# Newton norm groups spread over an attention tail, the order of head and tails, and an exponential of a constant behind three square roots

## Chip, core and metric

The kernel runs on one core of a Trainium2 chip. The metric is the device time of one execution in microseconds (us), lower is better. The engines of the core are PE (matrix multiplications and transpositions), DVE (vector), ACT (scalar: activations, copies, and the table loads that some activation functions need), POOL (a second, slower vector engine) and SP, which here only issues DMAs. Each engine works through its own list of instructions in order and waits at semaphores.

## What is computed

Four cross-attention layers run one after the other over 8 sequences of 128 rows by 256 columns, in float32. Each has projections, scores, a softmax and a weighted sum; L1, L2 and L3 end in an MLP with GELU. Of L0 the change touches only the first microseconds. What matters besides is the normalisation of rows, which stands in front of every part:

```
def layer_norm(x, w, b):
    mu = jnp.mean(x, axis=-1, keepdims=True)
    var = jnp.mean(jnp.square(x - mu), axis=-1, keepdims=True)
    return (x - mu) * jax.lax.rsqrt(var + EPS) * w + b
...
attn = jax.nn.softmax(scores, axis=-1)
out = jnp.einsum('bhqk,bhkd->bhqd', attn, v)
...
y = jax.nn.gelu(y @ fc_w + fc_b, approximate=True)
```

L1 uses a norm without the mean (`rmsnorm`, EPS 1e-06) between its attention and its MLP.

## The kernel before

The program is written as five instruction lists, one for each engine, that walk the same planned order of events. Projections in full precision are made of three fp32r products each (`three`, L768 to L770: high part by low, low by high, high by high), so every weight and every activation is split: ACT writes the rounded high part, DVE the rest. PE's general results go through two PSUM banks in turn, `ps` banks 6 and 7 ("general banks"): PE may fill one again only when the engines that read its last content are done, so the order of `j_bank` users on PE, ACT and DVE is one order.

**Head.** L0 runs in steps of 4 units. For a step, PE gathers stacked queries and keys (L1108 to L1111), ACT copies them (L1407), SP (for the first step ACT too) moves rows of the keys by DMA (L660), PE makes the scores (L1128), DVE takes maxima (L1816), POOL and a product with a rounded identity, `identR` (PE L1118), turn these into a correction, and PE and ACT make the exponentials (L1137, L1417). Rows, identity and a mask are loaded by three DMAs (L706 to L708) that SP issues behind the key moves of step 1. DVE waits for all three, adds a bias row to the values (L1806) and then writes `identR` (L1810).

**Attention of L1 and L3.** `att_order` lists units: 64 in L1 (4 iterations of 4 steps of 4), 32 in L3 (4 iterations of 4 steps of 2). A unit is: PE scores `S` (L897 in L1, L903 in L3), DVE maxima (L1619), ACT exponentials (L1274, which also sums), DVE reciprocal (L1570), POOL product (L1867), PE transposition `T` (L913), a copy by ACT (even units, L1285) or DVE (odd ones, L1632), and the product with the values `PV` (L936). There are two banks for scores and two for transpositions. Once for each step PE gathers queries `pq` (L855) and keys `pk` (L862, L865), which ACT (L1256, L1266) and DVE (L1616) write back. After an iteration ACT and DVE split the result (L1291, L1635) and the output projection `WO` follows; DVE adds it to the residual (L1641) and takes statistics (L1485).

**The norm** comes in three events: `nS` (DVE aggregates the statistics, L1496, and writes the variance; ACT takes the square root, L1214), `nX` (DVE reciprocal, L1505, and the scaled rows, L1508 or L1510, one instruction for each sequence) and `nT` for each pair of sequences (PE transposes, L802; ACT applies weight and bias, L1226 or L1228; DVE splits, L1524 and L1525). The square root and the exponential need different tables, as does GELU, so each switch has an `ACT_TABLE_LOAD` ahead of it. `GROUPS` says which pairs share an `nS`. The first group of the norm behind the attention, `L1r` in L1 and `L3nm` in L3, is worked in the attention's last units. There the table of extra events reads as follows (`total` is the number of units):

```
    first, rest, sqrt = {"L1": (total - 24, total - 4, 10), "L3": (10, total - 3, 5)}[ph]
...
    put(total - sqrt, "nS", after, 0)
    put(total - sqrt + 1, "nX", after, 0)
```

So `nS` comes in unit 54 of L1 and 27 of L3. The first MLP products `up` (12 products each; GELU on ACT L1369, split on DVE L1723 and L1724) stand in units `total`, `total + 1` and `total + 4`, among the last transpositions. Weights arrive in packs (DMA L690) and are split by `take` (ACT L1205, DVE L1475).

**Seams.** Before L2 (`L2n1`), in its middle (`L2n2`) and before L3 (`L3n1`) the last group's `nS` is the last square root ahead of exponentials; their table is loaded ahead of the first one (L1329 in L2, L1274 in L3). Keys and queries of L2 are written by ACT (L1312, L1306), scores are L988, maxima L1680, reciprocals L1688, transpositions L997.

## Time and profile before

| | us |
|---|---|
| three runs, median | 1166.39 |
| lowest, highest | 1165.26, 1166.6 |
| the profiled execution | 1168.75 |
| its span, first to last instruction | 1167.0 |
| PE busy, share of the span | 1061.5, 91% |
| DVE busy | 728.7, 62% |
| ACT busy | 716.2, 61% |
| POOL busy | 316.8, 27% |

The profiled execution is 0.20% above the median, and 1.75 us of it lie outside the span. PE is busy for most of the time; the parts where it is not are the head, the attention of L1 and L3 and the seams. The views used below are the timeline, which gives each instruction's start and length and the idle time ahead of it with its releaser; the chain of waits; and the busy time of all engines in a stretch, with the clock that TensorE was granted (1.00 is 2.4 GHz, 0.50 is 1.2 GHz).

### The profile page before, as it was taken

The page shows a single profiled execution, that of the slowest core. Times are in us where ns is not written, and L with a number is a line of the kernel's source. Part 1 is how long each engine was busy: PE and PEld are TensorE (multiplying, and loading weights), DVE is VectorE, ACT ScalarE, POOL GpSimd, SP SyncE. Part 2 cuts the span into 40 slices and gives each one's busy share as a digit, 9 for nine tenths or more (in the row PEclk, how much of TensorE's full clock was granted, in tenths as well). Part 3 has the DMA queues.
Part 4 walks back from the last instruction along what each step waited for, and adds up shares of the span by engine and source line. Part 5 has one row for each costly group of instructions (what it writes and reads, how often), then busy time and mean ns, then how long its engine had stood idle before and what let it go on. Part 6 is the DMA issues. An engine that isn't in the chain of part 4 may idle for free.

```text
span 1167.0 us, 24069 instructions
## 1 busy us (share of the span) xinstructions
PE 1061.5 (91%) x8248; PEld 936.3 (80%) x8248; DVE 728.7 (62%) x1755; ACT 716.2 (61%) x2080; POOL 316.8 (27%) x440
## 2 busy tenths in 40 slices
PE   7989897799979999999999979999999989778788
PEld 6767676577759889999998869999998979667588
DVE  6787584677786645555555645555555585767773
ACT  2777765677884465656655556565665552689852
POOL 5242533666540022211111103111111112243311
PEclk8999999899999999999999999999999999999899
DMA  5211111011101021111101001011111110100100
GB/s 169 70 43 46 24 33 42 16 29 25 44 26 46 19 91 46 47 46 47 46 17 71 28 22 45 25 46 46 46 46 37 32 60 1 49 17 19 48 10 28
DMA packets 29853, 48.09 MB, mean 41 GB/s; under 512 B 6627, under 2 KB 20389, under 8 KB 29734
## 3 DMA queue, kind: packets, MB, share of 16 engines
q1 hardware_dynamic: 29638, 46.49, 13.0%
q8 instruction: 68, 1.11, 0.4%
q14 instruction: 51, 0.42, 0.1%
q10 hardware_dynamic: 96, 0.07, 0.0%
HBM read 36.54 MB, written 1.05 MB: 32 GB/s over the span
## 4 chain that ended last, share of the span: by engine, by line
PE 65%; DVE 13%; ACT 10%; issue 7%; POOL 2%; SPq 1%; DMA 1%; ACTq 0%; DVEq 0%; POOLq 0%
PE ps L768 14%; PE ps L769 13%; PE ps L770 13%; PE ps L1012 4%; PE ps L988 4%; PE ps L1150 3%; ACT pt L1274 2%; PE ps L997 2%; DVE nm L1816 2%; PE ps L913 1%; DVE nmax L1619 1%; PE ps L1128 1%; PE ps L1137 1%; PE ps L936 1%; POOL pt L1867 1%
## 5 line engine op out<-in xcount | busy, mean ns | idle before, releaser
L1867 POOL TENSOR_TENSOR pt<-pt,prec 128x256 f32<-128x256 f32 (+1 forms) x224 | 181.3, 810 | 622.9 <-DVE prec L1688 501.1
L1329 ACT ACTIVATE pt<-ps,nmax 128x129 f32<-128x129 f32 x256 | 92.4, 367 | 100.7 <-DVE nmax L1680 99.9
L1475 DVE TENSOR_TENSOR rs<-wraw,rs 128x256 fp32r<-128x256 f32 (+2 forms) x116 | 68.7, 594 | 125.5 <-ACT rs L1205 125.1
L768 PE MATMUL ps<-rs 128*128 128x256 f32 x480 | 142.8, 298 | 4.1 <-DVE rs L1702 2.8
L769 PE MATMUL ps<-rs 128*128 128x256 f32 x480 | 135.9, 283 | 0.0
L770 PE MATMUL ps<-rs 128*128 128x256 f32 x480 | 135.8, 283 | 0.0
L1274 ACT ACTIVATE pt<-ps,nmax 128x256 f32<-128x256 f32 (+1 forms) x256 | 105.3, 425 | 40.3 <-DVE nmax L1619 39.9
L768 PE MATMUL ps<-ht,rs 128*128 128x256 f32 (+1 forms) x304 | 107.5, 354 | 9.0 <-DVE ht L1525 3.0
L770 PE MATMUL ps<-ht,rs 128*128 128x256 f32 (+1 forms) x304 | 100.9, 332 | 0.0
L769 PE MATMUL ps<-ht,rs 128*128 128x256 f32 (+1 forms) x304 | 100.9, 332 | 0.0
L768 PEld LDWEIGHTS ps<-rs 128*128 128x128 f32 x480 | 91.9, 191 | 7.9 <-DVE rs L1702 4.8
L1702 DVE SCALAR_TENSOR_TENSOR rs<-ps,col,rs 128x256 fp32r<-128x256 f32 x128 | 61.9, 483 | 53.4 <-ACT rs L1346 53.4
L769 PEld LDWEIGHTS ps<-rs 128*128 128x128 f32 x480 | 92.0, 192 | 0.0
L770 PEld LDWEIGHTS ps<-rs 128*128 128x128 f32 x480 | 91.9, 191 | 0.0
L768 PE MATMUL ps<-rs,ct 128*128 128x256 f32 x288 | 86.4, 300 | 3.4 <-ACT rs L1256 1.5
L1816 DVE TENSOR_REDUCE nm<-ps 128x2 f32<-128x512 f32 x128 | 82.6, 680 | 6.3 <-PE ps L1128 6.2
L988 PEld LDWEIGHTS ps<-fs 128*128 128x128 f32 x512 | 76.1, 191 | 10.2
L1619 DVE TENSOR_REDUCE nmax<-ps 128x2 f32<-128x512 f32 (+1 forms) x96 | 65.7, 685 | 29.5 <-PE ps L903 24.1
L1369 ACT ACTIVATE fs<-ps,col 128x256 f32<-128x256 f32 x96 | 40.2, 472 | 68.4 <-PE ps L770 67.2
L1417 ACT ACTIVATE pt<-ps 128x512 f32<-128x512 f32 x128 | 73.1, 599 | 13.3 <-PE ps L1137 11.6
L770 PE MATMUL ps<-rs,ct 128*128 128x256 f32 x288 | 80.9, 281 | 0.0
L769 PE MATMUL ps<-rs,ct 128*128 128x256 f32 x288 | 80.9, 281 | 0.0
(206 smaller groups left out, 2999.4 us busy)
## 6 DMA issues: line engine op xcount, KB each, us to landing
wraw<-in_packs SPq DMA_DIRECT2D x52, 512.0 KB, 3.7
rs<-rs SPq DMA_DIRECT2D x222, 32.0 KB, 1.9
bvr<-in_l2rows SPq DMA_DIRECT2D x16, 256.0 KB, 4.5
rs<-rs SPq DMA_DIRECT2D x96, 16.0 KB
row<-in_rows SPq DMA_DIRECT2D x2, 640.0 KB, 4.9
XH<-in_packs SPq DMA_DIRECT2D x2, 512.0 KB, 4.2
out<-X SPq DMA_DIRECT2D x4, 256.0 KB, 2.1
X<-in_x SPq DMA_DIRECT2D x3, 256.0 KB, 3.2
```

Of the source, the lines that this page charges most:

```text
L768: nc.tensor.matmul(dst, w[0], m[1], start=start, stop=False)
L769: nc.tensor.matmul(dst, w[1], m[0], start=False, stop=False)
L770: return nc.tensor.matmul(dst, w[0], m[0], start=False, stop=stop)
L988: last = nc.tensor.matmul(ps[:, S_BANK + g % 2, b * D:b * D + P + 1], qT[:, hh % 3, 2 * b2 + b, :], kT[:, hh % 3, 2 * b2 + b, :], start=Tr ...
L1274: last = nc.scalar.activation(prob[:, i % PROBS, h * keys:(h + 1) * keys], ps[:, SCORE_BANKS[ph][i % len(SCORE_BANKS[ph])], h * keys:(h + ...
L1329: last = nc.scalar.activation(prob[:, g % PROBS, k * D:k * D + P + 1], ps[:, S_BANK + g % 2, k * D:k * D + P + 1], ACT.Exp, bias=nmax[:, g ...
L1417: nc.scalar.activation(pt[:, i % L0_PTS, :], ps[:, L0_X[i % len(L0_X)], :], ACT.Exp, scale=Q0_SCALE).then_inc(Z["ex"], 1)
L1475: last = nc.vector.tensor_tensor(dst[1], src, f32(dst[0]), ALU.subtract)
L1619: nc.vector.tensor_reduce(nmax[:, i % 4, 0:nh], ps[:, SCORE_BANKS[ph][i % len(SCORE_BANKS[ph])], :].rearrange("p (h n) -> p h n", h=nh), A ...
L1702: nc.vector.scalar_tensor_tensor(cc[1][:, hd, two, :], ps[:, O_BANK + g % 2, 0:D].rearrange("p (b n) -> p b n", b=2), C(f"L2bv{p // PAIRS ...
L1816: nc.vector.tensor_reduce(nm[:, s % 3, im, 2 * p:2 * p + 2], ps[:, L0_S[i % len(L0_S)], :].rearrange("p (h n) -> p h n", h=2), AX.X, ALU.m ...
L1867: nc.gpsimd.tensor_tensor(pr, pr, prec[:, u % 4, 0:nh].unsqueeze(2).broadcast_to([P, nh, keys]), ALU.mult)\
```

## The change

1. **Newton roots.** For the first groups of `L1r` and `L3nm` (`ROOTS`) the square root on ACT and the reciprocal on DVE go. DVE computes 1/sqrt by itself: in `nS` two instructions that make a first guess from the bits of the number, and three rounds (`refine`) of three small instructions, each waiting for the one before. Two rounds stand in a new event `nR`, the third ahead of the first scaled rows.
2. **Spread.** `nX` of these groups is cut by pairs: in L1 `nS` in unit 54, `nR` in 55, pairs in 56, 57, 58 and their `nT` in 58, 60, 63 (before: 57, 60, 63); in L3 `nS` in 24, `nR` in 25, pairs in 26 and 27, `nT` in 27 and 29 (before `nS` in 27, `nX` in 28, `nT` in 30 and 31).
3. **Tails.** `up` 0, 1, 2 move from `total`, `total + 1`, `total + 4` to `total + 2`, `total + 4`, `total + 5`.
4. **Head.** SP issues the three loads behind the key moves of step 0 in place of step 1, and DVE writes `identR` ahead of the bias addition.
5. **Tables.** Behind the last square root of `L2n1`, `L2n2` and `L3n1` (`WARM`) ACT takes the exponential of one constant column into a tile that nobody reads, so that the table of the exponential is loaded there.

```diff
+ROOTS = {("L1r", 0), ("L3nm", 0)}
+ROOT_SEED = 0x5F3759DF - (1 << 30) - (1 << 22)
+WARM = {("L2n1", 1), ("L2n2", 1), ("L3n1", 1)}
...
-    first, rest, sqrt = {"L1": (total - 24, total - 4, 10), "L3": (10, total - 3, 5)}[ph]
+    first, rest = {"L1": (total - 24, total - 4), "L3": (10, total - 3)}[ph]
...
-    put(total - sqrt, "nS", after, 0)
-    put(total - sqrt + 1, "nX", after, 0)
-    for n, k in enumerate(GROUPS[after][0]):
-        put(total - sqrt + 3 + (3 if ph == "L1" else 1) * n, "nT", after, k)
+    sums, scale, turn = {"L1": (54, (56, 57, 58), (58, 60, 63)), "L3": (24, (26, 27), (27, 29))}[ph]
+    put(sums, "nS", after, 0)
+    put(sums + 1, "nR", after, 0)
+    for k in GROUPS[after][0]:
+        put(scale[k], "nX", after, 0, k)
+    for k in GROUPS[after][0]:
+        put(turn[k], "nT", after, k)
     for k in range(2):
-        put(total + k, "up", 0, k)
+        put(total + 2 + 2 * k, "up", 0, k)
         put(total + k, "w", f"{ph}w2_0", 2 * k, 2)
         put(total + 5 + k, "w", f"{ph}w2_1", 2 * k, 2)
-    put(total + 4, "up", 0, 2)
+    put(total + 5, "up", 0, 2)
...
                         if e == "pp":
                             key_blocks(i)
-                            if i == 1:
+                            if i == 0:
...
-                if e == "nS":
-                    act.wait_ge(n["stat"], k + 1)
+                if e == "nS" and (name, k) not in ROOTS:
+                    act.wait_ge(n["stat"], rooted(name, k))
...
+                if e == "nX" and (name, k) in WARM:
+                    nc.scalar.activation(warm[:, 0:1], eps[:, 0:1], ACT.Exp)
...
+            def refine(g):
+
+                link(nc.vector.tensor_tensor(sd[:, 2, g], sd[:, 3, g], sd[:, 3, g], ALU.mult))
+                link(nc.vector.tensor_tensor(sd[:, 2, g], sd[:, 2, g], sd[:, 0, g], ALU.mult))
+                link(nc.vector.scalar_tensor_tensor(sd[:, 3, g], sd[:, 2, g], 1.5, sd[:, 3, g], ALU.add, ALU.mult))
...
+                    if (name, k) in ROOTS:
...
+                        link(nc.vector.tensor_scalar(sd[:, 0, g], power, 1e-6 if name == "L1r" else 1e-5, -0.5, ALU.add, ALU.mult))
+                        link(nc.vector.tensor_scalar(sd[:, 3, g].bitcast(I32), sd[:, 0, g].bitcast(I32), -0.5, float(ROOT_SEED),
+                                                     ALU.mult, ALU.add))
...
+                elif e == "nR":
+                    refine(g)
+                    refine(g)
                 elif e == "nX":
...
+                    if (name, k) in ROOTS:
+                        if pair == GROUPS[name][k][0]:
+                            refine(g)
...
                         dve.wait_ge(d_in, 16 * 3)
+                        nc.vector.tensor_copy(identR, ident[:, :]).then_inc(ident_r, 1)
...
-                    if i == 0:
-                        nc.vector.tensor_copy(identR, ident[:, :]).then_inc(ident_r, 1)
```

The order of the instructions shows the change at three places. A name in brackets is a semaphore that the instruction waits for; `x3` means three more of the same.

**DVE in L1's last units.** Before, from the statistics on (`mv`, `sd` are statistics and factors, `nmax` the maxima of a unit, `prec` its reciprocals, L1508 the scaled rows):

```order
L1499 TENSOR_TENSOR sd<-mv 128x6 [waits vector_chain]
L1500 TENSOR_TENSOR sd<-sd,mv 128x6 [waits vector_chain]
L1619 TENSOR_REDUCE nmax<-ps 128x2 [waits L1_sm]
L1570 RECIPROCAL prec<-psums 128x2 [waits L1_nm,L1_ex]
L1505 RECIPROCAL sd<-sd 128x6 [waits L1r_sq]
L1508 TENSOR_SCALAR XH<-XH,sd 128x256 [waits vector_chain]
L1508 TENSOR_SCALAR XH<-XH,sd 128x256 x5
L1619 TENSOR_REDUCE nmax<-ps 128x2 [waits L1_sm]
L1570 RECIPROCAL prec<-psums 128x2 [waits L1_nm,L1_ex]
L1632 COPY pt<-ps 128x512 [waits L1_pm,L1_tm]
```

With the change (its own line numbers: L1524 and L1525 are the first guess, L1497 to L1499 a round, L1655 the maxima, L1544 the scaled rows):

```order
L1524 TENSOR_SCALAR sd<-sd 128x6 [waits vector_chain]
L1525 TENSOR_SCALAR sd<-sd 128x6 [waits vector_chain]
L1655 TENSOR_REDUCE nmax<-ps 128x2 [waits L1_sm,vector_chain]
L1606 RECIPROCAL prec<-psums 128x2 [waits L1_nm,L1_ex]
L1497 TENSOR_TENSOR sd<-sd 128x6
L1498 TENSOR_TENSOR sd<-sd 128x6 [waits vector_chain]
L1499 SCALAR_TENSOR_TENSOR sd<-sd 128x6 [waits vector_chain]
L1497 TENSOR_TENSOR sd<-sd 128x6 [waits vector_chain]
L1498 TENSOR_TENSOR sd<-sd 128x6 [waits vector_chain]
L1499 SCALAR_TENSOR_TENSOR sd<-sd 128x6 [waits vector_chain]
L1655 TENSOR_REDUCE nmax<-ps 128x2 [waits L1_sm,vector_chain]
L1606 RECIPROCAL prec<-psums 128x2 [waits L1_nm,L1_ex]
```

Further down stand the third round and two scaled rows, and the other four come in pairs behind the next two maxima. So seven instructions between one maximum and the next become six small ones, two more stand ahead of the first maximum, and three more and two rows ahead of the third.

**ACT in L3's last units.** Before, from the exponentials of unit 27 to those of unit 28 and what follows (L1274 exponentials, L1285 copy, L1291, L1256, L1266 results of `pq`, `pk` and the split):

```order
L1274 ACTIVATE pt,psums<-ps,nmax 128x128 [waits L3_tm,L3_mx]
L1274 ACTIVATE pt,psums<-ps,nmax 128x128 x3
L1285 COPY pt<-ps 128x512 [waits L3_pm,L3_tm]
L1214 ACT_TABLE_LOAD
L1214 ACTIVATE sd<-sd,eps 128x4 [waits L3nm_stat]
L1274 ACT_TABLE_LOAD [waits L3_tm]
L1274 ACTIVATE pt,psums<-ps,nmax 128x128 [waits L3_mx]
L1274 ACTIVATE pt,psums<-ps,nmax 128x128 x3
L1291 CAST rs<-ps 128x512 [waits L3_done,L3_pm]
L1256 ACTIVATE rs<-ps,col 128x512 [waits general_bank_filled,L3_sm]
L1266 CAST rs<-ps 64x2x128 [waits general_bank_filled,L3_sm]
L1274 ACTIVATE pt,psums<-ps,nmax 128x128 [waits L3_tm,L3_mx]
```

With the change (L1288 exponentials, L1299 copy, L1240 the affine step of a pair):

```order
L1288 ACTIVATE pt,psums<-ps,nmax 128x128 [waits L3_tm,L3_mx]
L1288 ACTIVATE pt,psums<-ps,nmax 128x128 x3
L1299 COPY pt<-ps 128x512 [waits L3_pm,L3_tm]
L1240 ACTIVATE XH<-ps,col 128x256 [waits general_bank_filled]
L1240 ACTIVATE XH<-ps,col 128x256
L1288 ACTIVATE pt,psums<-ps,nmax 128x128 [waits L3_tm,L3_mx]
L1288 ACTIVATE pt,psums<-ps,nmax 128x128 x3
L1305 CAST rs<-ps 128x512 [waits L3_done,L3_pm]
L1270 ACTIVATE rs<-ps,col 128x512 [waits general_bank_filled,L3_sm]
L1280 CAST rs<-ps 64x2x128 [waits general_bank_filled,L3_sm]
L1288 ACTIVATE pt,psums<-ps,nmax 128x128 [waits L3_tm,L3_mx]
L1288 ACTIVATE pt,psums<-ps,nmax 128x128 x3
```

Two table loads and a square root went, and the affine step of the first pair, before behind unit 30, stands in their place.

**ACT at the seam into L2.** Before (L1214 square root, L1310 and L1312 a key block, L1226 affine steps):

```order
L1214 ACTIVATE sd<-sd,eps 128x2 [waits L2n1_stat]
L1310 ACTIVATE fs<-ident,col 128x4 [waits general_bank_filled]
L1312 ACTIVATE fs<-ps,col 128x4x128
L1226 ACTIVATE XH<-ps,col 128x256 [waits general_bank_filled]
L1226 ACTIVATE XH<-ps,col 128x256
L1205 CAST rs<-wraw 128x1024 [waits pack_loaded0,L1m_out]
L1306 ACTIVATE fs<-ps,l2q 128x512 [waits general_bank_filled]
L1226 ACTIVATE XH<-ps,col 128x256 [waits general_bank_filled]
```

With the change (L1229 is the exponential of the constant):

```order
L1226 ACTIVATE sd<-sd,eps 128x2 [waits L2n1_stat]
L1324 ACTIVATE fs<-ident,col 128x4 [waits general_bank_filled]
L1326 ACTIVATE fs<-ps,col 128x4x128
L1229 ACT_TABLE_LOAD
L1229 ACTIVATE warm<-eps 128x1
L1240 ACTIVATE XH<-ps,col 128x256 [waits general_bank_filled]
L1240 ACTIVATE XH<-ps,col 128x256
L1217 CAST rs<-wraw 128x1024 [waits pack_loaded0,L1m_out]
L1320 ACTIVATE fs<-ps,l2q 128x512 [waits general_bank_filled]
L1240 ACTIVATE XH<-ps,col 128x256 [waits general_bank_filled]
```

The load that stood ahead of the first L1329 now stands between the key block and the affine step.

## Rows read from the trace of the kernel before

**Rows 1.** The page: its head line, and its chain of work that ended last, by engine.

```profile
span 1167.0 us, 24069 instructions
...
PE 65%; DVE 13%; ACT 10%; issue 7%; POOL 2%; SPq 1%; DMA 1%; ACTq 0%; DVEq 0%; POOLq 0%
```

**Rows 2.** The chain of waits in the head, in order of time: start, us, what.

```profile
18.68 3.90 DMA mraw<-in_mask_s
```

**Rows 3.** Timeline of the head: start, us, engine, line, operation, count, [idle before].

```profile
13.13 4.40 SPq L660 DMA_DIRECT2D rs<-rs  x6
...
22.70 0.49 DVE L1806 TENSOR_TENSOR fs<-ps,row 128x128 f32<-128x128 f32 x2 [1.63 <-DMA mraw<-in_mask_s]
...
23.66 0.69 PE L1118 MATMUL ps<-rs 128*128 128x128 f32 x2 [2.77 <-DVE rs L1810]
...
24.91 0.29 PEld L1128 LDWEIGHTS ps<-rs 128*128 128x128 f32 x1 [0.33 <-DMA rs<-rs]
```

**Rows 4.** Busy time by stretch: us, PE, PEld, DVE, ACT, POOL, granted clock, DMA share, GB/s.

```profile
24.00:30.00 6.00, 6.00 (x23) 5.24 (x23) 5.63 (x14) 2.06 (x4) 0.65 (x3) 0.51 0.65 205
...
1094.00:1102.00 8.00, 4.99 (x33) 3.78 (x34) 5.23 (x11) 8.00 (x35) 2.47 (x3) 0.57 0.01 3
1112.00:1120.00 8.00, 6.01 (x42) 5.81 (x43) 5.08 (x9) 2.51 (x6) 2.06 (x2) 0.79 0.01 2
```

**Rows 5.** Timeline, last units of L1's attention: DVE and ACT.

```profile
324.16 0.68 DVE L1619 TENSOR_REDUCE nmax<-ps 128x2 f32<-128x512 f32 x1
...
324.60 1.28 ACT L1274 ACT_TABLE_LOAD   x1
...
324.83 0.17 DVE L1505 RECIPROCAL sd<-sd 128x6 f32<-128x6 f32 x1
...
325.04 2.46 DVE L1508 TENSOR_SCALAR XH<-XH,sd 128x256 f32<-128x256 f32 x6
325.89 0.47 ACT L1274 ACTIVATE pt<-ps,nmax 128x256 f32<-128x256 f32 x1
...
327.42 0.68 DVE L1619 TENSOR_REDUCE nmax<-ps 128x2 f32<-128x512 f32 x1
```

**Rows 6.** Timeline, end of L1's attention on PE.

```profile
351.30 0.64 PE L936 MATMUL ps<-pt,fs 128*32 128x128 f32 x16 [2.25 <-DVE pt L1632]
...
356.37 0.36 PE L768 MATMUL ps<-ht,rs 128*128 128x256 f32 x1
```

**Rows 7.** Timeline, seam from L1's MLP to L2.

```profile
407.80 0.67 ACT L1312 ACTIVATE fs<-ps,col 128x512 f32<-128x512 f32 x1
...
411.85 0.47 PE L768 MATMUL ps<-ht,rs 128*128 128x512 f32 x1
```

**Rows 8.** Timeline, second half of L2 begins.

```profile
693.34 1.28 ACT L1329 ACT_TABLE_LOAD   x1
...
698.57 0.46 PE L997 MATMUL ps<-ident,pt 128*128 128x128 f32 x2 [1.84 <-POOL pt L1867]
```

**Rows 9.** Timeline, first unit of L3's attention.

```profile
1011.13 0.69 DVE L1619 TENSOR_REDUCE nmax<-ps 128x4 f32<-128x512 f32 x1 [1.72 <-PE ps L903]
```

**Rows 10.** Timeline, last units of L3's attention: ACT and PE.

```profile
1090.84 1.28 ACT L1214 ACT_TABLE_LOAD   x1
...
1092.44 1.28 ACT L1274 ACT_TABLE_LOAD   x1
...
1093.74 0.37 ACT L1274 ACTIVATE pt<-ps,nmax 128x128 f32<-128x128 f32 x1
...
1097.01 0.77 PE L903 MATMUL ps<-rs 128*128 128x256 f32 x2 [4.24 <-DVE rs L1616]
...
1101.60 0.41 ACT L1274 ACTIVATE pt<-ps,nmax 128x128 f32<-128x128 f32 x1
```

**Rows 11.** Timeline, end of L3's attention on PE.

```profile
1113.99 0.42 PE L936 MATMUL ps<-pt,fs 128*32 128x128 f32 x8 [2.31 <-DVE pt L1632]
...
1118.81 0.28 PE L768 MATMUL ps<-ht,rs 128*128 128x256 f32 x1
```

More of the change, by code:

```diff
@@ L100, with rooted @@
           "L3n1": ((0, 1, 2), (3,)), "L3nm": ((0, 1), (2, 3))}
+ROOTS = {("L1r", 0), ("L3nm", 0)}
+ROOT_SEED = 0x5F3759DF - (1 << 30) - (1 << 22)
+WARM = {("L2n1", 1), ("L2n2", 1), ("L3n1", 1)}
 NORMS = ["ctx", "lat", "L1r", "L2n1", "L2n2", "L2nm", "L3n1", "L3nm"]
+def rooted(name, k):
+    return sum((name, j) not in ROOTS for j in range(k + 1))
 def first_order():
@@ L458, in build @@
         eps = sb("eps", [P, 2])
+        warm = sb("warm", [P, 1])
         nm = sb("nm", [P, 3, 2, 4])
@@ L1487, in stats, with norm_step @@
                     link(last)
-            def norm_step(e, name, k):
+            def norm_step(e, name, k, pair=None):
                 n = N[name]
-                if e in ("nS", "nX"):
+                if e in ("nS", "nR", "nX"):
                     src = XH if name == "L1r" else X
```

18 lines of the change are left out of this document (12 added, 6 removed).

## Prediction

> **What bounds the kernel.** First the page: a span of 1167.0 us, and a chain that ended last of which PE has 65%, DVE 13%, ACT 10% [rows 1]. PE is the limit almost everywhere, so an edit pays only where PE stands still, or runs at the lower clock, and only as much as that. I went through the chain of waits and then the timeline at the places that the diff touches. What the reader is to see there: in the head PE stands 2.77 us for `identR` [rows 3]; in the tails of L1's and L3's attention ACT or DVE is full while PE waits, up to 4.24 us at once [rows 10]; at the seams PE waits for short chains through ACT and DVE. The stretches view adds the clock: 0.51 in the head's 24 to 30, 0.57 and 0.79 in L3's tail [rows 4].
>
> The sum is made against the profiled span of 1167.0; that execution took 1168.75, 0.20% above the median of 1166.39, to which I apply the difference unscaled.
>
> **Head.** Before, SP issues six key moves from 13.13 to 17.53 [rows 3], then the three loads, the last at 18.68 with 3.90 us to land [rows 2]; DVE is idle 1.63, goes on at 22.70, and PE at 23.66 [rows 3]. With the loads behind two moves, they start 4 × 4.40/6 = 2.9 us earlier (the estimate counts SP's own wait for step 1 as issue time). `identR` is done before the bias work, so PE could go on about 2 us earlier. The price: key moves of step 1 are issued some 1.3 us later by SP and queue behind the large row load. What is late next is the transfer for step 2, which even now holds PE's weight load until 24.91 [rows 3]. It is issued only a few tenths earlier, since it waits for ACT's stacks. So the gain at 24.91 is 0.3 to 0.9 us; it can grow behind that, as PE was at half clock from 24 to 30 with a busy share of 6.00 in 6.00 [rows 4], but DVE was busy 5.63 of these 6.00 and would catch it at once. I take **-1.0**, bounds -2.5 (DVE's idle time of 1.63 and the transfer's 0.9) and 0 (the step 1 moves take it all back).
>
> **L1's tail.** Removed on ACT: a load (1.28), a square root, a load (1.28) [rows 5]. But look at who is late. The maxima of unit 55 end at 324.84, the exponential starts at 325.89, so the loads cost 1.0 there, and the maxima of unit 56 come at 327.42 only because DVE was scaling six rows for 2.46 us [rows 5]. DVE is the limit for four units. A linked small instruction costs 325.04 - 324.83 = 0.21 us from start to start [rows 5]. Added are 2 + 9 of them, 2.3 us, less one reciprocal of 0.21: **2.1 us more on DVE**, and the 2.46 us of scaling stay. I moved the timeline on: exponentials of unit 55 at 325.3 (0.6 earlier), of 56 about 0.8 earlier, then of 57 some 0.8 later, because third round and two rows stand ahead of its maxima, and the carry at unit 63 is 1.1 late (0.5 to 1.3).
>
> The end is reordered. Before, two `up` groups of some 1.45 us each stand among the last transpositions; the last copy is late on DVE, and PE idles 2.25 us until 351.30 [rows 6]. Now they stand behind the last transposition, one of them behind the last `PV`, so `PV` comes about 1.2 earlier with the carry in, but one more `up`, and the split ahead of `WO`, follow it. The point that I compare is the group that began at 356.37 [rows 6]: it comes 0.8 late by my hand. L1's tail: **+0.8**, bounds -1.5 (DVE's additions fit into its idle time) and +2.5 (two loads' worth comes back as a carry of all 2.1 us).
>
> **L3's tail.** The same edits, but here ACT is the limit: 8.00 busy of 8.00 us [rows 4]. The loads at 1090.84 and 1092.44, with the root between them, hold the exponentials of unit 28 until 1093.74: the removed piece is 1093.74 - 1090.84 = 2.9 us [rows 10]. Guess and first rounds move to units 24 and 25, where DVE has idle time; third round and two rows (0.6 + 0.7) stand ahead of the maxima of 27 and hold it 0.9. The affine step of pair 0 (two instructions, 1.0) now stands ahead of the exponentials of 28, that of pair 1 ahead of 30. By hand: exponentials of 28 start 1.0 earlier, PE's unit 30, which waits 4.24 until 1097.01, 0.55 earlier, those of 31 within 0.2 of 1101.60 [rows 10], but now both affine steps lie behind ACT and not ahead. From there no `up` stands between the last transpositions and no split ahead of the last copies: the last `PV`, at 1113.99 after 2.31 us idle [rows 11], comes at about 1108.4 to 1109; then `up`, split and `WO`, two `up`, and the group that began at 1118.81 [rows 11] begins at about 1114.3, 4.5 earlier. The old stretch had clock 0.79 [rows 4]; the new one has emptier time before its products, and I give 0.5 back for that. **-4.0**, bounds -5.5 and -1.5.
>
> **Seams.** The load is 1.28 and the exponential of one column some 0.2, together 1.5, moved ahead of affine steps. At L2n1, ACT's key block ends at 408.47 (407.80 + 0.67) and the affine step follows at once; DVE's split, its value block and PE's group at 411.85 [rows 7] hang on it one behind another: **+1.6** there. The load taken away later stood beside a PE that was busy; I find 0.4 of idle time behind it. Net **+1.2**, bounds 0 and +3.0 (the low clock follows the new gap). At L2n2 the load at 693.34 is in the chain that ends in 1.84 us of PE idle at 698.57 [rows 8]; ACT has room behind its root, so **-1.0**, bounds -2.7 and 0. At L3n1 the maxima end at 1011.82 [rows 9], when the old load was just through: **0**, to +0.3.
>
> Here the Trainium skill speaks to the load. The trace first: 324.60 plus 1.28 is 325.88, and the exponential starts at 325.89 [rows 5]. The page "ScalarE: Activation LUTs", section "What ACT_TABLE_LOAD costs", gives a load of about 1283 ns and a drain of about 1380 ns behind it for every switch. By that each of the four loads removed would give back 1.4 us more; the trace has the first figure and not the second, and it decides.
>
> The skill also speaks against the change. The page "VectorE: DVE Perf Modes", section "Rules for kernel authors", says of chained operations to keep their number small, not their semaphores. By that rule eleven small operations are the wrong coin for one square root. My terms above already charge each by its row.
>
> **Sum.** -1.0 + 0.8 - 4.0 + 1.2 - 1.0 + 0 = -4.0: 1166.4 - 4.0 = **1162.4 us** (0.34% faster; the span 1163.0). A measurement of this kernel can tell about 0.2%, 2.3 us, from no change.
>
> **Rivals.**
> - *The gaps go and the clock stays up* (0.20). The low clock of the head [rows 4] follows an idle PE; if that gap is short, the products there run at full rate. Head -2.5, L1 -1.0, L2n1 0.5, L2n2 -2.5, L3 -5.0: -10.5, **1155.9**. Against it: a transfer still holds PE at 24.91.
> - *The expected gain is given back behind it* (0.22). DVE's linked instructions hold the maxima in both tails, and the end of L3 hangs on copies that queue on DVE: head -0.5, L1 +1.5, L2n1 +1.2, L2n2 -0.5, L3 -2.5: -0.8, **1165.6**.
> - *Slower: the low clock moves onto dense products* (0.09). Before, much of it fell on stretches where ACT was the limit (0.57 with ACT full [rows 4]). With the `up` groups behind the last transposition PE is emptier ahead and then has 6 us of products in a row, which at half rate cost 3 more, in L1 and in L3, and 2 at the new gap of L2n1: 8 against -4.0, **1170.4**. It decides if at least three such stretches fall there.
> - *The constant's exponential loads nothing, or a load stays ahead of the exponentials as well* (0.01): the instruction order shows one load, at the new place. Only the seams would be off, by 1 us.
>
> **Chances.** Forecast 0.48, rivals 0.20, 0.22, 0.09, 0.01. Faster by over 0.2%: 0.44 of the forecast's 0.48, 0.20, 0.03 of the second: **0.67**. Slower by over 0.2%: **0.08** (third rival nearly whole). Within: **0.25**. The range for 8 in 10 takes in most of the first two rivals: **1155.5 to 1167.0**. The forecast's own is 1159 to 1165.
>
> **What would show it.** In the new trace: PE goes on in the head before 22.5 and waits for the transfer near 24.4; between the maxima of units 55 and 56 of L1 six instructions 0.21 apart, and maxima of 57 later than before; in L3 no load between exponentials, PE's wait at unit 30 under 4 us, last `PV` to the group behind `WO` and two `up` more than 5 us; at L2n1 about 1.5 us more idle ahead of the group that stood at 411.85; at L2n2 under 1 us in place of 1.84. The forecast is wrong if linked instructions cost clearly more than 0.21, if L3's last `PV` is not at least 4 us earlier, or if the clock's low stretches fall on the `up` groups.

## The result and the profile after

The changed kernel took **1168.71 us** (median of 20 runs, 1166.41 to 1172.34) against 1165.89 (20 runs, 1163.54 to 1169.45): ratio 1.0026, 95% interval 1.0018 to 1.0035, or 3.0 us slower (2.1 to 4.1). The forecast was 4.0 us faster, with a range that ended at 1167.0. It was wrong in its sign. Here and below, the us beside a ratio are the ratio's share of the time of before; they can differ from the plain difference of the medians, in most kernels by under 0.7, at most by 1.3.

The profiled execution of the changed kernel took 1168.0, of that of before 1168.75. So the two traces say -0.8 where the medians say +2.8. The profiled execution of before was 2.9 us above the median of its kernel. A comparison of the two traces has to go part by part, and I measure each part between two events that both kernels have.

**Whole.** The page of the changed kernel: head line, and the chain of work that ended last by engine. Against [rows 1] DVE has one point more in the chain, PE two less.

```profile
span 1166.2 us, 24089 instructions
...
PE 63%; DVE 14%; ACT 9%; issue 8%; POOL 2%; SPq 2%; DMA 1%; DVEq 0%; ACTq 0%; POOLq 0%
```

**Head.** Timeline of the changed kernel (start, us, engine, line, operation, [idle before <- releaser]). PE takes up `identR`'s product at 21.81, where it stood until 23.66 [rows 3]. The wait for a transfer at 23.65 comes about as forecast. But two more follow, one for each further step, and at 32.16 PE waits 1.77 us for key rows.

```profile
21.81 0.41 PE L1130 MATMUL ps<-rs 128*128 128x128 f32 x2 [0.43 <-POOL rs L1972]
...
23.65 0.50 PE L1140 MATMUL ps<-rs 128*128 128x512 f32 x1 [0.84 <-DMA rs<-rs]
...
27.30 0.50 PE L1140 MATMUL ps<-rs 128*128 128x512 f32 x1 [0.80 <-DMA rs<-rs]
32.16 0.50 PE L1140 MATMUL ps<-rs 128*128 128x512 f32 x1 [1.77 <-DMA rs<-rs]
```

In this trace the clock does not fall in the head. The stretch 24 to 30, at 0.51 in [rows 4], now reads:

```profile
24.00:30.00 6.00, 5.20 (x35) 4.45 (x33) 5.68 (x14) 4.26 (x8) 1.12 (x5) 1.00 0.62 190
```

**L1's tail.** DVE from the maxima (L1655) of unit 55 to those of 57, then POOL's two products in that piece. This answers to [rows 5].

```profile
322.03 0.69 DVE L1655 TENSOR_REDUCE nmax<-ps 128x2 f32<-128x512 f32 x1
322.64 0.15 DVE L1606 RECIPROCAL prec<-psums 128x2 f32<-128x2 f32 x1
322.71 0.14 DVE L1497 TENSOR_TENSOR sd<-sd 128x6 f32<-128x6 f32 x1
322.89 1.04 DVE L1498 TENSOR_TENSOR sd<-sd 128x6 f32<-128x6 f32 x1
323.96 0.17 DVE L1499 SCALAR_TENSOR_TENSOR sd<-sd 128x6 f32<-128x6 f32 x1
324.16 0.17 DVE L1497 TENSOR_TENSOR sd<-sd 128x6 f32<-128x6 f32 x1
...
324.76 0.69 DVE L1655 TENSOR_REDUCE nmax<-ps 128x2 f32<-128x512 f32 x1
...
326.03 0.63 DVE L1497 TENSOR_TENSOR sd<-sd 128x6 f32<-128x6 f32 x1
...
327.10 0.61 DVE L1544 TENSOR_SCALAR XH<-XH,sd 128x256 f32<-128x256 f32 x2
327.63 0.68 DVE L1655 TENSOR_REDUCE nmax<-ps 128x2 f32<-128x512 f32 x1
```

```profile
322.87 1.04 POOL L1902 TENSOR_TENSOR pt<-pt,prec 128x512 f32<-128x512 f32 x1 [3.08 <-DVE prec L1606]
325.60 1.04 POOL L1902 TENSOR_TENSOR pt<-pt,prec 128x512 f32<-128x512 f32 x1 [1.70 <-DVE prec L1606]
```

The linked instructions start 0.20 us apart, as forecast, but two of them last 1.04 and 0.63: the first starts 0.02 behind a POOL product and ends with it, the second starts in the middle of one and ends with it too. The third round and the first two rows take 326.03 to 327.63, 1.60 us, all of it ahead of the maxima of unit 57. What comes out on PE at the end of L1's attention (L948 is `PV`, L925 the transposition; [rows 6] is its old form), and the busy time by stretch (us, PE, PEld, DVE, ACT, POOL, granted clock, DMA share, GB/s):

```profile
345.88 1.08 PE L948 MATMUL ps<-pt,fs 128*32 128x128 f32 x16 [2.21 <-DVE pt L1668]
346.89 1.12 PE L925 MATMUL ps<-ident,pt 128*128 128x128 f32 x4
...
350.50 1.08 PE L948 MATMUL ps<-pt,fs 128*32 128x128 f32 x16
```

```profile
344.00:351.50 7.50, 5.62 (x48) 4.63 (x48) 3.62 (x7) 3.27 (x6) 0.13 (x1) 0.54 0.53 175
351.50:358.00 6.50, 6.42 (x55) 6.20 (x52) 5.45 (x11) 3.41 (x8) 0.00 (x0) 1.00 0.01 3
```

**Seams.** At L2n1 the load stands ahead of the affine step (L1240), and PE waits for that; at L2n2 the load is gone from between maxima and exponential, and the 1.84 us of [rows 8] are 0.99:

```profile
409.21 1.28 ACT L1229 ACT_TABLE_LOAD   x1
...
410.51 0.20 ACT L1229 ACTIVATE warm<-eps 128x1 f32<-128x1 f32 x1
410.62 1.00 ACT L1240 ACTIVATE XH<-ps,col 128x256 f32<-128x256 f32 x2
...
411.76 0.36 PE L780 MATMUL ps<-rs,ct 128*128 128x256 f32 x1 [0.76 <-ACT XH L1240]
...
698.52 0.44 PE L1009 MATMUL ps<-ident,pt 128*128 128x128 f32 x2 [0.99 <-POOL pt L1902]
```

**L3's tail.** PE's waits, against 4.24 of [rows 10] and 2.31 of [rows 11], and the clock. The row at 1111.48 holds the last two `PV`; that of unit 31, whose old start is 1113.99, starts at 1111.91. The stretch ahead of them holds the first `up` group (L780 to L782), at half clock.

```profile
1097.34 0.48 PE L915 MATMUL ps<-rs 128*128 128x256 f32 x2 [0.92 <-issue]
...
1104.71 0.63 PE L925 MATMUL ps<-ident,pt 128*128 128x128 f32 x4 [1.63 <-ACT pt L1299]
...
1107.02 1.09 PE L925 MATMUL ps<-ident,pt 128*128 128x128 f32 x4 [1.33 <-DVE pt L1668]
...
1111.48 1.08 PE L948 MATMUL ps<-pt,fs 128*32 128x128 f32 x16
```

```profile
1106.00:1110.00 4.00, 2.98 (x18) 2.29 (x19) 2.77 (x5) 1.76 (x2) 0.00 (x0) 0.50 0.36 122
1110.00:1114.00 4.00, 4.00 (x36) 3.36 (x34) 1.50 (x3) 1.43 (x3) 0.00 (x0) 0.67 0.00 0
```

### The profile page after: what moved, and what is told of

Same layout as the page of the kernel before. It is cut to its first block, busy times and chain, and to the rows that moved or that the text cites. A ratio compares the mean times of both kernels' runs of the same rounds, so it can differ in the third digit from the quotient of the medians.

```text
span 1166.2 us, 24089 instructions
## 1 busy us (share of the span) xinstructions
PE 1061.7 (91%) x8248; PEld 934.7 (80%) x8248; DVE 733.4 (63%) x1774; ACT 710.9 (61%) x2077; POOL 316.7 (27%) x440
## 3 DMA queue, kind: packets, MB, share of 16 engines
HBM read 36.54 MB, written 1.05 MB: 32 GB/s over the span
## 4 chain that ended last, share of the span: by engine, by line
PE 63%; DVE 14%; ACT 9%; issue 8%; POOL 2%; SPq 2%; DMA 1%; DVEq 0%; ACTq 0%; POOLq 0%
PE ps L780 14%; PE ps L781 13%; PE ps L782 13%; PE ps L1024 4%; PE ps L1000 4%; PE ps L1162 3%; ACT pt L1288 2%; PE ps L1009 2%; DVE nm L1851 2%; PE ps L925 2%; DVE nmax L1655 2%; PE ps L948 1%; POOL pt L1902 1%; PE ps L1149 1%; SPq L672 1%
## 5 line engine op out<-in xcount | busy, mean ns | idle before, releaser
L780 PE MATMUL ps<-rs 128*128 128x256 f32 x480 | 142.5, 297 | 4.7 <-DVE rs L1738 2.8
L782 PE MATMUL ps<-rs 128*128 128x256 f32 x480 | 135.7, 283 | 0.0
L1288 ACT ACTIVATE pt<-ps,nmax 128x256 f32<-128x256 f32 (+1 forms) x256 | 105.1, 423 | 49.3 <-DVE nmax L1655 48.6
L780 PE MATMUL ps<-ht,rs 128*128 128x256 f32 (+1 forms) x304 | 107.2, 353 | 6.4 <-DVE ht L1561 3.0
L782 PE MATMUL ps<-ht,rs 128*128 128x256 f32 (+1 forms) x304 | 100.7, 331 | 0.0
L780 PEld LDWEIGHTS ps<-rs 128*128 128x128 f32 x480 | 91.7, 191 | 9.0 <-DVE rs L1738 4.8
L782 PEld LDWEIGHTS ps<-rs 128*128 128x128 f32 x480 | 91.7, 191 | 0.0
L780 PE MATMUL ps<-rs,ct 128*128 128x256 f32 x288 | 86.5, 300 | 3.3 <-ACT fs L1326 1.4
L1655 DVE TENSOR_REDUCE nmax<-ps 128x2 f32<-128x512 f32 (+1 forms) x96 | 65.7, 685 | 28.5 <-PE ps L915 23.3
L782 PE MATMUL ps<-rs,ct 128*128 128x256 f32 x288 | 80.9, 281 | 0.0
```

The source lines that it names most:

```text
L780: nc.tensor.matmul(dst, w[0], m[1], start=start, stop=False)
L782: return nc.tensor.matmul(dst, w[0], m[0], start=False, stop=stop)
L1288: last = nc.scalar.activation(prob[:, i % PROBS, h * keys:(h + 1) * keys], ps[:, SCORE_BANKS[ph][i % len(SCORE_BANKS[ph])], h * keys:(h + ...
L1655: nc.vector.tensor_reduce(nmax[:, i % 4, 0:nh], ps[:, SCORE_BANKS[ph][i % len(SCORE_BANKS[ph])], :].rearrange("p (h n) -> p h n", h=nh), A ...
```

## Experiments: the four parts, each alone

Each kernel is the kernel before with one part of the diff. All four ran on one chip beside 26 runs of the kernel before. The diffs of the first two stand against the kernel before, all later ones against the changed kernel.

**Head alone.**

```diff
-                            if i == 1:
+                            if i == 0:
                                 sp.dma_start(row[...], rows[0].partition_broadcast(P)).then_inc(d_in, 16)
```

> The kernel before with the head's part of the change alone: three loads behind two key moves, identR cast ahead of the bias work; nothing else. My prediction's step: -1.0 us, bounds -2.5 and 0. Theory (each part costs what it does, and parts add): -1 to -2.5, because in the two traces POOL's work of the head's third step is 2.3 us earlier. Rival (the gain is only a low stretch of the clock that fell elsewhere, since two steps later just 0.4 us are left): 0 within 0.5 us, and a trace in which the third step is early and the fifth is not.

1167.43 (11 runs) against 1166.8: ratio 1.0004, 0.9996 to 1.0013, +0.5 us. The rival holds. There are twenty traces in all, one for each kernel of this document. In the six kernels with this part the third step's first work on POOL comes 2.9 us earlier than in before's trace, in the fourteen without it 0.3 earlier. At the fifth step it is 0.7 against 0.4, and at L1's first `WO` 1.4 against 1.7. So 2.5 us at the third step are 0.3 at the fifth and nothing behind.

**Constants alone.**

```diff
+                if e == "nX" and (name, k) in WARM:
+                    nc.scalar.activation(warm[:, 0:1], eps[:, 0:1], ACT.Exp)
```

> The kernel before with the exponential of a constant behind the root of L2n1, L2n2 and L3n1 alone. Prediction's steps: +1.2 - 1.0 + 0 = +0.2 us. Theory from the two traces: L2n1 +1.5, L2n2 -3.1, L3n1 +0.8, so -0.8, between -2 and +0.5. Rival (the -3.1 at L2n2 was a low stretch of the clock that fell elsewhere and not the load): L2n2 about -1 and the whole +1 to +1.5.

1166.09 (12 runs) against 1166.8: 0.9999, 0.9986 to 1.0012, -0.1 us. Half shown, by lengths between the same two events in all twenty traces. L2n1, from the last MLP output of L1 to the first maxima of L2: +1.51 to +1.53 in the six with it, 0.00 to +0.03 in the fourteen without. L2n2, from the maxima 60 to 72 of L2: the waits above give 0.85 at the seam. But eight of the eleven traces with it are shorter by 3.6 and three by 2.1 to 2.3 (mean -3.2). The nine without it run from +0.1 to -2.8 (mean -1.2). So L2n2 is worth 2.0 in the mean: 0.85 for the load, and the rest, as I read it, because fewer low stretches of the clock fall there; the shortest lengths with and without it, -3.6 and -2.8, differ by 0.8, the load alone.

**L1's tail alone** and **L3's tail alone.** Each is points 1 to 3 of the change for one phase.

```diff
-ROOTS = {("L1r", 0), ("L3nm", 0)}
+ROOTS = {("L1r", 0)}
```

> The kernel before with L1's tail alone changed: Newton steps of L1r's first group in place of the square root, scaled pair by pair, its three transposes and the three up groups moved back. Prediction's step: +0.8 us. Theory from the two traces: +3.4, because DVE's additions carry 1 to 1.6 us to the last unit and the first up group runs at half clock from 344.6 on, which adds 1.5 to 2. Rival (the half clock there was a chance of that one execution): +1 to +1.6, and a trace whose up groups run at full clock.

> The kernel before with L3's tail alone changed in the same way. Prediction's step: -4.0 us. Theory from the two traces: WO of the last iteration 2.8 us earlier, of which the up groups that follow it at half clock give back 2: -0.7, between -1.5 and 0. Rival (the half clock there was caused further ahead, by L3n1's new place, whose low stretch began at 1010.2): with L3n1 as before the whole part gives -2.5 to -4.

L1's: 1172.78 (5 runs), 1.0051, 1.0038 to 1.0064, **+6.0 us**. L3's: 1163.92 (8 runs), 0.998, 0.9968 to 0.9991, **-2.3 us**. Neither theory foresaw 6. The half clock in L1 was there again, from 345.3. For L3 the trace is the rival's: its `up` groups run at full clock (1.00 in 1106 to 1110), and -2.3 is nearer to its -2.5 than to the theory's -0.7. But L3n1 is not the cause, since a later kernel with L3's tail and without L3n1 has the half clock on the `up` groups. The four parts add up to +4.1, the whole measured +3.0. L1's tail alone turns the result.

## Experiments: the halves of the two tails

Here the roots and the place of the `up` groups are taken apart, all on one chip beside 35 runs of before.

```diff
-        put(total + 2 + 2 * k, "up", 0, k)
+        put(total + (2 + 2 * k if ph in ("L3", ) else k), "up", 0, k)
-    put(total + 5, "up", 0, 2)
+    put(total + (5 if ph in ("L3", ) else 4), "up", 0, 2)
```

> The kernel before with L1's Newton steps, pairwise scaling and moved transposes, but with the three up groups where they stood before. Theory (the whole of L1's tail costs 6 us, of which the additions on DVE carry 1.5 to 2 to the last unit, and the rest comes from the up groups behind the last transposition, at half clock): +1.5 to +2.5 us. Rival (it is DVE: its additions, held by POOL's products, are all of the cost): +4 to +6. Prediction's step for this half: +1.1.

> The kernel before with L1's three up groups moved back alone; square root and loads as before. Theory: +3 to +4.5 us, with a low stretch of the clock on the first up group or the last products before WO. Rival (DVE is all of it): 0 to +1. Prediction's step for this half: 0.8 - 1.1 = -0.3.

> The kernel before with L3's Newton steps and moved transposes, but with the up groups where they stood. Prediction's step: the loads that go free 0.2 to 0.5 us at the last units, so -0.5. Rival (the 2.9 us of loads and root come back whole, as ACT is the limit there): -2.0 to -3.

> The kernel before with L3's three up groups moved back alone; square root and loads as before. Prediction's step: most of L3's gain is this order, -2.5 to -3.5. Theory after the first four runs (whole tail -2.3 to -2.9): -1.5 to -2.5. Rival (the loads are all of the gain): 0 to -0.5, or slower as in L1.

| | median (12 runs each) | ratio, 95% | us |
|---|---|---|---|
| L1, roots | 1169.38 | 1.0022, 1.0009 to 1.0034 | +2.6 |
| L1, `up` groups | 1165.91 | 0.9998, 0.9986 to 1.0011 | -0.2 |
| L3, roots | 1165.19 | 0.9990, 0.9977 to 1.0003 | -1.2 |
| L3, `up` groups | 1168.15 | 1.0021, 1.0006 to 1.0036 | +2.5 |

Of these, L1's roots come out about as the theory had them. The others do not. L1's `up` groups alone cost nothing, where the theory had 3 to 4.5. L3's roots lie between the prediction's step and the rival. L3's `up` groups alone, which the prediction had as most of the gain, make it slower. In L1 the halves add up to 2.4 of 6.0, in L3 to +1.3 where the whole is -2.3, so they do not act one by one.

The traces are sharper than these times where DVE or ACT sets the pace: with L1's roots the exponentials of unit 63 start 1.64 to 1.66 later than before in all seven kernels that have two rounds, with L3's those of unit 31 1.04 to 1.06 later in all twelve. With the old units the spread is wider. In L1 the twelve kernels that have them put unit 63 at -0.18 to +0.54, the two latest where the granted clock is 0.50 and 0.59 in 326 to 332. Start against before's trace, in us, L1 counted from `WO` of iteration 2, L3 from that of iteration 1:

| | L1 exp. of unit 63 | L1 last `PV` | L3 exp. of unit 28 | of unit 31 | L3 last transposition | L3 last `PV` |
|---|---|---|---|---|---|---|
| roots | +1.66 | +1.66 | -0.58 | +1.05 | -1.53 | -1.54 |
| `up` groups | +0.01 | -0.26 | -0.21 | -0.22 | -1.70 | -0.29 (half clock) |
| both | +1.65 | +1.88 (half clock) | -0.60 | +1.04 | -3.44 | -4.14 |

The last column is the `PV` of unit 31. Where a row of PE's timeline reads `x16` in L3, it holds the `PV` of units 30 and 31, 8 records each, and the second starts later than the row. Both halves together reach -4.14 at full clock (L3's tail alone), and -2.04 at half clock (the changed kernel).

In L1 the roots carry 1.65 us to the last unit, whatever the order; against the twelve kernels with old units it is 1.1 to 1.8, in the mean 1.5. The `up` groups behind the last transposition alone let the last `PV` start only 0.25 earlier, and one more group of 1.43 us now stands behind it. In L3 the transpositions stood behind the `up` groups on PE, and the two edits together bring the last `PV` 4.1 earlier. The row of the `up` groups hides as much: this is its transposition of unit 31 and its last two `PV`, with the clock.

```profile
1109.57 1.08 PE L932 MATMUL ps<-ident,pt 128*128 128x128 f32 x4 [3.81 <-DVE pt L1675]
...
1114.03 1.08 PE L955 MATMUL ps<-pt,fs 128*32 128x128 f32 x16
```

```profile
1110.00:1114.00 4.00, 4.00 (x24) 3.09 (x22) 1.32 (x3) 0.00 (x0) 0.00 (x0) 0.50 0.00 0
```

The 4.46 us between the two starts are 2.56 at full clock, as a later kernel shows. So at full clock the `up` groups alone would give about -2.4, an estimate, and much of the +2.5 can be the clock.

## Experiments: the parts within the whole, and the clock

**The change with L1's tail as before, and with L1's `up` groups alone as before.**

> The changed kernel with L1's tail as before (head, exponentials of a constant and L3's tail changed). Theory (L1's tail is what makes the change slower, and costs what it did alone, 6 us): -3.1 us against before, as head +0.6, constants -0.7, L3's tail -2.9 measured alone. Rival (L1's tail costs only the 2.3 us that the traces show between WO of iteration 2 and the first MLP output, and the rest was chance): +0.5 us, 2.3 below the change's +2.8.

> The changed kernel with L1's three up groups alone put back where they stood. Theory (DVE's additions carry 1.6 us to the last unit whatever the order is, and the order costs more on top): 1 to 2.5 us under the changed kernel, so +0.3 to +1.8 against before. Rival (the order costs nothing, as it measured alone): as the changed kernel, +2.8.

1166.80 (12 runs) against 1168.02: 0.9988, 0.9973 to 1.0002, -1.4 us. The second: 1168.54, 1.0003, 0.9992 to 1.0015, +0.4. From +3.0 that makes 4.4 for L1's tail within the change, of which the roots are 1.8 and the order 2.6. These are differences of kernels that ran at other times than the changed one, beside other runs of before, and each is good to about 1.5. The first theory's place is right, its size lies between the two; in the second the theory's range is met.

**The change with products of the identity in PE's waits.**

```diff
+FILL = {('T', 'L1', 62): 8, ('PV', 'L1', 30): 16, ('T', 'L3', 30): 10, ('T', 'L3', 31): 9}
                 elif e == "T":
+                    fill(ps[:, OUT_BANKS[ph][0], :], FILL.get(("T", ph, i), 0))
                     pe.wait_ge(a["nm"], i + 1)
```

> The changed kernel with products of the identity, whose result nobody reads, on PE where it waits ahead of the last transposes and products of both tails: 8 and 16 in L1, 10 and 9 in L3. Theory (the low clock falls on the up groups because PE stands idle ahead of them; each such stretch costs up to 2 us): no low stretch on the up groups of either tail, last products of L3 up to 2.0 us and of L1's end up to 1.4 us earlier, together 2 to 3.4 us under the changed kernel, so -0.6 to +0.8 against before. Rival (the clock falls with the work ahead of the tail, not with this idle time): as the changed kernel or 0.5 above it, and low stretches on the up groups as before.

1171.05 (12 runs): 1.0033, 1.0018 to 1.0048, +3.9 us, no gain, and outside both forecasts. I had taken 0.12 us for a product; PE's timeline of this kernel has two records for each, and 3.74 us for the 16, longer than the wait of 2.21 that they were to fill:

```profile
345.11 3.74 PE L791 MATMUL ps<-ident 128*128 128x128 f32 x32
348.78 0.65 PE L951 MATMUL ps<-pt,fs 128*32 128x128 f32 x16
349.35 0.66 PE L927 MATMUL ps<-ident,pt 128*128 128x128 f32 x4
351.36 0.64 PE L951 MATMUL ps<-pt,fs 128*32 128x128 f32 x16
```

```profile
348.00:351.50 3.50, 3.50 (x45) 3.04 (x47) 0.71 (x2) 0.03 (x1) 0.00 (x0) 1.00 0.68 214
```

It still tells what the half clock costs in L1, for this end ran at full clock. From one `PV` to the last transposition and on to the last `PV`, with an `up` group in between, PE works without a gap: 0.57 + 2.01 = 2.58 us here, 1.01 + 3.61 = 4.62 in the changed kernel. So the clock takes **2.0 us** there, and the fills' own delay ate what they won: the first MLP output of L1 came 3.20 later than in before's trace, 3.39 in the changed kernel. Taking the 2.0 off, the new tail would be 1.4 longer than before's, 0.25 less than the carry of 1.65, so the order by itself costs nothing at full clock. In L3 the fills pushed the transpositions back.

**The parts that gained:** L3's tail and L2n2's constant, then the same with the `up` groups of L3 as before, the same with L1's tail added, and the same with shorter fills in L3.

```diff
-WARM = {("L2n1", 1), ("L2n2", 1), ("L3n1", 1)}
+WARM = {("L2n2", 1)}
```

> The kernel before with L3's tail changed and the exponential of a constant behind L2n2's root alone, head, L1's tail, L2n1 and L3n1 as before: the parts that gained. Theory (parts add: L3's tail -2.9 and L2n2 -0.8): -3.7 us. Rival (parts shift the clock's low stretches onto one another and do not add): -1 to -2.5.

> The kernel before with L3's Newton steps (up groups as before) and L2n2's exponential of a constant. Theory (L3's order of up groups gains only where the clock stays up, which it does in one trace of five): -2.5 to -3 against before, no worse than with the order changed. Rival (the order gains 2 us on the whole, as alone it cost 2.4 and together with Newton the tail gained 2.3): -1.

> The kernel before with L3's tail, L2n2's exponential of a constant and L1's tail changed; it differs from the kernel with the first two alone (-2.0 us as a median of 12) by L1's tail. Theory A (L1's tail costs what the traces show between WO of iteration 2 and the first MLP output, 2.4 us, and 0.3 in L2): +0.5 against before. Theory B (it costs the 5.9 us that it measured alone): +3.5. In the trace: last products of L1's attention 1.6 to 2.0 us later than before, counted from WO of iteration 2, the first MLP output 3.2 to 3.4 later.

```diff
+FILL = {('T', 'L3', 29): 3, ('T', 'L3', 30): 6, ('T', 'L3', 31): 3}
```

> The kernel before with L3's tail and L2n2's exponential of a constant changed, and 3, 6 and 3 products of the identity on PE ahead of the last three transposes of L3, less than its wait there is long. Theory (the low stretch on the first up group comes from PE's idle time ahead of it and costs 2.0 us at the last products): no low stretch there, last products 4.2 us earlier than before counted from WO of iteration 1, where four of five traces had 2.2; 1 to 2 us under the same kernel without them, so -3 to -4 against before. Rival (the clock falls anyway): -2 and a low stretch between 1100 and 1110 as before.

| | median | before | ratio, 95% | us |
|---|---|---|---|---|
| L3's tail, L2n2 | 1165.76 | 1168.02 | 0.9984, 0.9972 to 0.9996 | -1.9 |
| `up` of L3 as before | 1164.69 | 1165.59 | 0.9993, 0.9984 to 1.0003 | -0.8 |
| L1's tail added | 1169.19 | 1165.59 | 1.0030, 1.0020 to 1.0039 | +3.5 |
| short fills | **1162.85** | 1165.59 | 0.9976, 0.9965 to 0.9986 | **-2.8** |

The first two came out as their rivals had them (-1 to -2.5, and -1): the parts that gained do not add up. L1's tail costs 5.4 here (+3.5 less -1.9, measured on two chips): theory B, and the same size as the 6.0 and 4.4 before. With the fills the kernel is the fastest of this case against its own runs of before. That it beats the same kernel without them the times do not settle, but the traces tell why it should: the low stretch is gone, as its theory had it, though the time stays short of the theory's -3 to -4. First the kernel without fills: transpositions of units 30 and 31 and the last two `PV`, with the clock. Then the kernel with them: the fills ahead of unit 31, its transposition and the last two `PV`:

```profile
1100.98 0.63 PE L932 MATMUL ps<-ident,pt 128*128 128x128 f32 x4 [1.63 <-ACT pt L1306]
...
1103.30 1.08 PE L932 MATMUL ps<-ident,pt 128*128 128x128 f32 x4 [1.33 <-DVE pt L1675]
...
1107.76 1.08 PE L955 MATMUL ps<-pt,fs 128*32 128x128 f32 x16
```

```profile
1098.00:1106.00 8.00, 4.67 (x41) 3.17 (x42) 5.51 (x12) 4.89 (x13) 2.45 (x2) 0.79 0.20 66
1106.00:1110.00 4.00, 4.00 (x32) 3.36 (x32) 1.23 (x3) 1.43 (x3) 0.00 (x0) 0.56 0.00 0
```

```profile
1099.53 0.94 PE L798 MATMUL ps<-ident 128*128 128x128 f32 x6
1100.93 0.63 PE L934 MATMUL ps<-ident,pt 128*128 128x128 f32 x4 [0.46 <-DVE pt L1678]
...
1103.49 0.65 PE L958 MATMUL ps<-pt,fs 128*32 128x128 f32 x16
```

```profile
1098.00:1106.00 8.00, 7.20 (x75) 5.61 (x74) 6.01 (x12) 4.91 (x9) 1.41 (x1) 1.00 0.20 68
1106.00:1110.00 4.00, 3.72 (x31) 3.72 (x32) 3.26 (x7) 1.70 (x5) 0.00 (x0) 1.00 0.00 0
```

From the transposition of unit 31 to the last two `PV` it is 4.46 us without and 2.56 with fills; at full clock that piece is 1.9 shorter. The length of L3's tail, from `WO` of iteration 1 to the first MLP output, shows two values in the kernels that have this tail without fills. It is -0.4 to -0.7 against before where the low clock falls on the first `up` group (the changed kernel and three others) and -2.7 where it does not (two). All four traces that have fills in L3 run the last `PV` at full clock, and two of the six without. That speaks for PE's idle time as the cause, but with ten traces chance is not excluded.

**The short fills in the changed kernel**, and **12 more of them in L1's old tail.**

> The changed kernel with the 3, 6 and 3 products of the identity in L3's tail and nothing else. Theory (the low stretch on L3's first up group, there in the changed kernel's trace, comes from PE's idle time and costs 2.0 us): last products of L3 4.2 us earlier than before, counted from WO of iteration 1, in place of 2.3, and 1 to 2 us under the changed kernel: +0.8 to +1.8 against before. Rival (the gain beside it was chance): +2.8, and a low stretch on the up groups.

> The kernel before with L3's tail, L2n2's exponential of a constant and the 3, 6 and 3 products of the identity in L3's tail, and 12 more of them in L1's tail ahead of its last product, where PE waits 2.25 us. Theory (in L1's unchanged tail the low stretch that falls on WO and the up groups in about half the traces costs 1 to 2 us, and comes from that wait): no low stretch after 340 in L1, and 0.5 to 1 us under the same kernel without the 12, so -3.3 to -3.8 against before. Rival (the products only move the stretch to the next gap): -2.7 and a stretch later, in L1's MLP or the seam.

1167.63 (12 runs) against 1167.04: 1.0002, 0.9989 to 1.0015, +0.2 us, 2.8 under the changed kernel, more than the theory's 1 to 2. The last `PV` of L3 is 3.8 earlier than before in place of 2.0, and the stretch 1106 to 1110, which had 0.50, has 1.00:

```profile
1106.00:1110.00 4.00, 4.00 (x43) 3.27 (x44) 3.83 (x8) 2.67 (x5) 1.31 (x1) 1.00 0.40 131
```

So the low clock on L3's `up` groups took about 2 us of the change's gain. The kernel with the 12: 1164.42 (12 runs), 0.9982, 0.9970 to 0.9994, -2.1 us. The theory's gain did not come: its clock is 1.00 from 338 to 362, but so it is up to 358 in the kernel without the 12, and again the fills were longer (12 of 0.23 us, 2.8) than the wait of 2.25, so that the last `PV` of L1 came 0.35 later than its unit 63. It was the same mistake of size as before, and settles nothing on L1's clock.

**Two more rounds of Newton in L1**, roots alone otherwise.

```diff
                 elif e == "nR":
-                    refine(g)
-                    refine(g)
+                    for _ in range(4):
+                        refine(g)
```

> The kernel before with L1's Newton steps, up groups as before, and four rounds of Newton at their first place in place of two: six more linked instructions on DVE. Theory (each costs 0.20 to 0.21 us and DVE is the limit there, so what is added is carried to the last unit): exponentials of the last unit 1.65 + 1.2 to 1.3 us later than before, counted from WO of iteration 2, and about +1.2 us on the time above the kernel with two rounds (+2.4), so +3.6. Rival (DVE has room ahead of the later units): exponentials of the last unit 1.65 later as with two rounds.

1170.14 (8 runs) against 1165.59: 1.0037, 1.0022 to 1.0051, +4.3 us. The exponentials of the last unit start 2.84 later than before: 1.65 plus 1.19 for six instructions, 0.20 each, carried in full. The rival falls. What is put on DVE there arrives at the last unit. The last `PV` starts 4.39 later; the other 1.55 come behind unit 63, where this trace has a low stretch on the first `up` groups in their old place:

```profile
346.00:350.00 4.00, 4.00 (x24) 4.00 (x24) 2.69 (x5) 2.83 (x5) 0.29 (x1) 0.61 0.40 131
```

## Why the prediction was wrong

**L1's tail: forecast +0.8, measured +6.0 alone, 4.4 and 5.4 within others.** Here the sign was lost, in three terms.
- *The carry.* I forecast 1.1 us (0.5 to 1.3) at unit 63; it is 1.65 against before's trace, 1.5 against the mean of the twelve kernels with old units. The instructions cost 0.20 as priced, but two were held beside POOL's product, by 0.87 and 0.46. The rows that gave the price [rows 5] show one with no product beside it. So the maxima of unit 56 came at the old time and not 0.8 earlier, and those of 57 1.6 late.
- *The clock.* I wrote that `PV` comes "about 1.2 earlier with the carry in". It comes 1.9 later. At full clock it would be level with before, and half of that miss is the carry; 2.0 is the half clock on the first `up` group and its neighbours. In the sum for L1 it had no term at all: I had it only in the third rival. All three traces of this tail without fills in either tail have it there from start to end of the group (0.50 in 347 to 350.5 in two, in 348 to 352 in the third, whose tail stands later), the old tail only now and then.
- *What is left.* Between `WO` of iteration 2 and the first MLP output the new tail is 3.15 (four traces) and the old 0.99 (ten traces) above before's trace, so 2.2. L2's second half is 0.3 longer in the seven traces that have L1's roots with two rounds, and not in the one with four; why is open. That makes 2.5 of 4.4 to 6.0, and it is less than 1.65 + 2.0, since old tails too meet a low stretch at their end, in five of ten traces. Where the rest lies is open. In the trace of L1's tail alone, L2n2 is 1.4 longer than the mean of the kernels with the old table load there, and L3's tail about 1 longer than in the other old ones, both places where the clock scatters; one trace can't tell whether L1's tail brings that about. The mean granted clock over the timed runs gives more time at half clock where L1's tail is added to L3's tail and L2n2 (48.4 us against 42.7, on two chips), but not where it stands alone against before (47.3 against 47.7).

**L3's tail: forecast -4.0, measured -2.3.** The mechanism was right, two sizes were off. ACT's first exponentials behind the removed loads start 0.60 earlier, not 1.0, PE's unit 30 starts 0.4 later and not 0.55 earlier, and the last `PV` is 4.1 earlier at full clock where 5 were forecast. Then the clock: I gave back 0.5 for it, and it takes 2.0 in four of six traces. My own signs for a wrong forecast came true: the clock's low stretches fell on the `up` groups, and in the changed kernel L3's last `PV` is 2.04 earlier and not 4. The third rival named the mechanism, at 0.09, with 3 us each in L1 and L3 and 2 at L2n1. It is 2.0 in each tail and nothing at L2n1, where all six traces agree to 0.02. L1's 2.0, the 1.5 beyond what I gave back in L3, and the carry's miss of 0.55 take back the forecast's 4.0. The rest of the way to +3.0 is the head's 1.0 that did not come, and what is open above. The third rival was right in kind, and its 1170.4 is nearer to 1168.71 than my 1162.4.

**Head: forecast -1.0, measured +0.5 (-0.5 to +1.5).** The step "it can grow behind that" failed. I looked for what is late next at one step; behind it stand the transfers of the next two, the last of which holds PE 1.77 us.

**Constants: forecast +0.2, measured -0.1.** L2n1 was forecast +1.6 at the seam and is +1.52; the 0.4 to be found behind it was not there. L2n2 was -1.0: 0.85 for the load and 1.2 more for the clock, within its bounds. For L3n1, from the last MLP output of L2 to `WO` of iteration 1, +0.7 with and +0.4 without, inside the scatter.

**The base.** I added up against a profiled execution 0.20% above the median and called the difference unscaled. Against the mean of the other traces, before's own is 1.7 longer in L0 and 1.2 in L2n2, but 1.0 shorter at the end of L1's attention. A clock term read from one trace, as the head's 0.51 and the waits at L2n2 were, is a draw.

## What to carry over

Dense products that are gathered behind a stretch in which PE idles can run at the lower clock: price them at both levels before moving them there, as two groups here cost 2.0 us each that way. A small instruction on a vector engine costs what its row says only if the row stood beside the same work of the neighbour. On an engine that sets the pace of a chain, every 0.20 us arrives at its end. And where PE idles ahead of dense products, a few products without a use, shorter in all than the wait, can pay: in L3 the traces give them about 2 us.
